# A post-norm decoder layer on one core: a new order of work in the joined cross-attention and routing loop

## The chip, the cores and the metric

The program runs on one NeuronCore of one Trainium2 chip. The metric is the time of one execution on the device, in microseconds (us). Engines are named as in the profile: PE is TensorE's matmuls and PEld its weight loads, DVE is VectorE, ACT is ScalarE, POOL is GpSimd, SP is SyncE, which only issues DMAs.

## The reference, cut to what matters

Batch 64, sequence 64, width 256: 4096 tokens, all fp32.

```python
x = layernorm(x + attn(x))                    # 16 heads, ALiBi, causal
# cross attention: K = V source ctx, scores summed over the batch
A = maximum(abs(masked_scores.sum(0)), 1)     # one matrix for all tokens
O = einsum('hst,bthe->bshe', A, ctx @ Wh)
Y = (O - mean(O)) / sqrt(var(O) + 1e-3) * gamma + beta
x = layernorm(x + (relu(x @ wg) * Y) @ wo)
# feed-forward: 64 experts, top 6 of a softmax router, plus a shared expert
topk_w, topk_idx = top_k(softmax(x @ gate_w.T), 6); topk_w /= sum(topk_w)
routed = sum_k topk_w[k] * (silu(x @ w1[k].T) @ w2[k].T)
g, u = split(x @ shared_gate_up.T, 2)         # 352 columns each
x = layernorm(x + routed + (silu(g) * u) @ shared_down.T)
```

## The kernel before, in words

The 4096 tokens are 32 tiles of 128 (NT = 32). The program has four stages, one after the other: self-attention with the sums of the cross-attention scores (up to 315 us), a joined loop that finishes the cross-attention, norms, routes, runs the shared expert and scatters the rows to pages in HBM (315 to 777 us), the experts page by page (804 to 1284 us), and the combination of the six results with the last norm.

The change lies in the joined loop. Every engine has a list of stages, each with a lag: the helper `tiles` (line 109) walks over steps s, and at step s an engine runs each stage of its list, in the order of the list, for tile s minus its lag. So the list is the order of an engine's queue, written out by hand; semaphores (`ev(name, t)` waits until tile t's event has been counted) tie the engines together. Loops are unrolled four steps deep.

PE's stages (lines 641 to 722), in the order of the list before, with their lags: `c_z_gate` (0), cross-attention product and gate; `ranks` (3), counting of chosen experts; `c_transpose` (1) of the normed group output, line 666; `shared_up` (3), 12 fp32 matmuls of the shared expert's gate and up halves, line 708, in the profile 24 records; `x2_transpose` (2), line 682; `c_project` (1), line 674; `c_out` (0), line 658; `router` (2), line 690; `shared_down` (4), line 718. 

The two norms of the loop share one power on POOL: `pair_rstd` (line 1041) takes for tile t the group norm's variance of t and the second norm's of t - 1, waits for `gn_nm` and `ln2_nm`, makes the power (line 1047) and then mean times power (line 1050, `pair_sh`); ACT applies both (`group_apply`, line 894, and `apply2`, line 904). POOL's queue then has `scatter` (line 1055): six indirect DMAs of the tile with lag 4 (line 1064), which wait for that tile's `ln2_done`, `dest_done` and `tope_done`.

On DVE, `gated` (line 1258) feeds `c_project`; `residual2` (line 1265), `sums2`, `mean2` and `pair_in` (lines 1241, 1242) turn its result into the second norm's statistics; `group_sums` and `group_mean` do the same for the group norm; `shared_gate` (line 1362) and `shared_mul` (line 1368) are the shared expert's gate; `page_...` (lines 1309 to 1349) and `top6...` (lines 1280 to 1303) are the routing, `add_shared` (line 1374) adds the shared expert. On ACT, `x2t_evac` (line 920) copies the transposed row for `router` and `shared_up`, `th_g` (line 949) is the Tanh of the gate half. SP loads `cn` four tiles ahead (line 459).

## Time and profile before

| | us |
|---|---|
| three runs, not profiled | 1398.18, 1401.5, 1402.94 |
| median | 1401.5 |
| the profiled execution | 1399.86 |
| its span | 1398.0 |
| joined loop, 315 to 777 | 462 |
| busy in the span: PE, DVE, POOL, ACT | 1016.2, 785.7, 565.1, 416.3 |

The span is the time from the first to the last instruction that the profile shows; the profiled execution's own time is 1.86 us longer. A record of POOL's indirect DMA is its issue, not its transfer. "Remote" and "another core or an unknown queue" are names for a releaser that the profile could not find among the instructions; this program has one core. The mean granted clock over the span is 0.852, where 1.00 is 2.4 GHz and 0.50 is 1.2 GHz.

### The profile page before, as it was taken

The page shows a single profiled execution, that of the slowest core. Times are in us where ns is not written, and L with a number is a line of the kernel's source. Part 1 is how long each engine was busy: PE and PEld are TensorE (multiplying, and loading weights), DVE is VectorE, ACT ScalarE, POOL GpSimd, SP SyncE. Part 2 cuts the span into 40 slices and gives each one's busy share as a digit, 9 for nine tenths or more (in the row PEclk, how much of TensorE's full clock was granted, in tenths as well). Part 3 has the DMA queues.
Part 4 walks back from the last instruction along what each step waited for, and adds up shares of the span by engine and source line. Part 5 has one row for each costly group of instructions (what it writes and reads, how often), then busy time and mean ns, then how long its engine had stood idle before and what let it go on. Part 6 is the DMA issues. An engine that isn't in the chain of part 4 may idle for free.

```text
span 1398.0 us, 32488 instructions
## 1 busy us (share of the span) xinstructions
PE 1016.2 (73%) x9108; PEld 867.2 (62%) x9108; DVE 785.7 (56%) x2447; ACT 416.3 (30%) x1061; POOL 565.1 (40%) x780
## 2 busy tenths in 40 slices
PE   5699999977776777677765498889888888885000
PEld 4588887867675667566764376678676766673000
DVE  5477777754444444444443365556555555552996
ACT  3355555533232323232321022222222222221121
POOL 0122222221454545454546034456444545553454
PEclk9899999987888878887877589999999999997555
DMA  6455555530221212121132065567555555642994
GB/s 204 146 173 171 171 175 182 180 91 24 76 70 67 70 66 70 66 70 66 67 97 102 24 183 163 166 199 215 179 173 176 184 167 181 195 145 101 300 315 170
DMA packets 136190, 197.13 MB, mean 141 GB/s; under 512 B 18397, under 2 KB 111062, under 8 KB 136152
## 3 DMA queue, kind: packets, MB, share of 16 engines
q1 hardware_dynamic: 68200, 104.04, 24.3%
q10 hardware_dynamic: 47920, 41.09, 10.4%
q0 software_dynamic: 20032, 51.55, 10.1%
q8 instruction: 18, 0.29, 0.1%
q14 instruction: 20, 0.16, 0.0%
HBM read 105.76 MB, written 95.03 MB: 144 GB/s over the span
## 4 chain that ended last, share of the span: by engine, by line
PE 53%; another core or an unknown queue 16%; issue 10%; ACT 7%; DVE 6%; ACTq 4%; DMA 1%; POOL 1%; DVEq 1%; SPq 0%; POOLq 0%
PE psum L746 7%; PE psum L769 7%; PE psum L534 5%; PE psum L718 4%; PE psum L750 4%; PE psum L763 3%; PE psum L779 3%; PE psum L593 3%; PE psum L523 2%; PE psum L547 2%; PE psum L649 2%; PE psum L558 2%; ACTq L969 2%; PE psum L690 1%
## 5 line engine op out<-in xcount | busy, mean ns | idle before, releaser
L1082 POOL DMA_INDIRECT expert_results<-arena,udest x224 | 237.8, 1062 | 278.9 <-issue 227.8
L1064 POOL DMA_INDIRECT expert_rows<-row,dest x192 | 186.9, 973 | 69.1 <-issue 67.9
L1461 DVE COPY arena<-arena 128x896 f32 x224 | 129.4, 640 | 90.1 <-PE psum L750 63.1
L746 PE MATMUL psum<-arena 128*128 128x256 f32 x448 | 129.2, 438 | 60.7 <-ACT arena L983 49.6
L746 PEld LDWEIGHTS psum<-arena 128*128 128x128 f32 x448 | 92.0, 216 | 80.5 <-ACT arena L983 54.0
L1443 DVE COPY arena<-psum 128x512 f32<-128x512 f32 x112 | 72.1, 686 | 82.0 <-remote 45.4
L769 PE MATMUL psum<-arena 128*128 128x128 f32 x896 | 117.5, 285 | 0.0
L769 PEld LDWEIGHTS psum<-arena 128*128 128x128 f32 x896 | 106.7, 195 | 9.9 <-issue 9.9
L1035 POOL TENSOR_TENSOR xnb<-xn,c_bout 128x256 f32<-128x256 f32 x32 | 23.3, 727 | 219.8 <-DVE ln_r L1167 207.7
L690 PE MATMUL psum<-c_wgate,x2t 128*128 128x64 f32 x128 | 28.6, 364 | 107.0 <-ACT x2t L920 98.9
L974 ACT ACTIVATE arena<-psum 128x512 f32<-128x512 f32 x56 | 33.5, 597 | 237.4 <-PE psum L750 160.5
L718 PE MATMUL psum<-c_sdn,arena 128*128 128x256 f32 x192 | 82.6, 595 | 20.2 <-DVE arena L1368 17.8
L1362 DVE SCALAR_TENSOR_TENSOR arena<-arena,psum 128x384 f32<-128x384 f32 x32 | 17.7, 554 | 141.4 <-ACT arena L949 131.9
L690 PEld LDWEIGHTS psum<-c_wgate,x2t 128*128 128x128 f32 x128 | 23.6, 260 | 113.0 <-ACT x2t L920 82.9
L1047 POOL TENSOR_TENSOR pair_rs<-pair_ve,mhalf 128x2 f32<-128x2 f32 x33 | 23.6, 717 | 173.2 <-DVE pair_nm L1242 170.6
L708 PE MATMUL psum<-x2t,c_sgu 128*128 128x128 f32 x768 | 91.4, 276 | 0.0
L708 PEld LDWEIGHTS psum<-x2t,c_sgu 128*128 128x128 f32 x768 | 88.7, 193 | 0.0
L718 PEld LDWEIGHTS psum<-c_sdn,arena 128*128 128x128 f32 x192 | 53.1, 294 | 31.8 <-DVE arena L1368 18.2
L949 ACT ACTIVATE arena<-psum 128x384 f32<-128x384 f32 x32 | 15.7, 490 | 178.7 <-remote 173.3
L534 PE MATMUL psum<-xt,c_wqkv 128*128 128x128 f32 x512 | 68.4, 289 | 0.0
L779 PE MATMUL psum<-c_ident,arena 128*128 128x128 f32 x448 | 60.1, 276 | 11.3 <-DMA arena<-expert_rows 10.1
L750 PE MATMUL psum<-arena 48*128 48x256 f32 x448 | 66.3, 416 | 0.0
(204 smaller groups left out, 2188.8 us busy)
## 6 DMA issues: line engine op xcount, KB each, us to landing
expert_rows<-zeros SPq DMA_DIRECT2D x64, 536.0 KB, 4.8
arena<-expert_rows ACTq DMA_DIRECT2D x224, 134.0 KB
arena<-in_w_experts SPq DMA_DIRECT2D x64, 448.0 KB
arena<-expert_results SPq DMA_DIRECT2D x32, 768.0 KB, 5.2
xn<-in_x SPq DMA_DIRECT2D x32, 128.0 KB, 2.1
cbt<-in_ctx_t SPq DMA_DIRECT2D x32, 128.0 KB, 4.7
cn<-in_ctx SPq DMA_DIRECT2D x32, 128.0 KB
xt<-in_x_t ACTq DMA_DIRECT2D x30, 128.0 KB, 4.7
```

Of the source, the lines that this page charges most:

```text
L534: q = pe.matmul(ps[m], wqkv[:, c, col:col + P], xt[u][:, c, :], start=c == 0, stop=c == 1)
L690: q = pe.matmul(ps_lg, x2t[u][:, c, :], wgate[:, c, :], start=c == 0, stop=c == 1)
L708: q = pe.matmul(ps[:, m, :], sgu[:, c, col:col + P], x2t[u][:, c, :], start=c == 0, stop=c == 1)
L718: q = pe.matmul(ps_sd, sh[u][:, m, :], sdn[:, m, :], start=m == 0, stop=m == SC - 1)
L746: pe.matmul(ps_uy[:, v, :], uhm[:, 4 * u + v, :], uw[:, 4 * u + v, 2 * (IM + IQ) + D:UW], start=True, stop=False)
L750: m = pe.matmul(ps_uy[:, v, :], uhr[own, 2 * u + v // 2, :], uw[own, 4 * u + v, 2 * (IM + IQ):2 * (IM + IQ) + D], start=False, stop=True)
L769: m = pe.matmul(ps_hm[:, v * P:(v + 1) * P], uw[:, 4 * u + v, c * (IM + IQ):c * (IM + IQ) + IM], uxt[:, 8 * u + 2 * v + c, :], start=c == ...
L779: m = pe.transpose(ps_ux[:, v // 2, (2 * (v % 2) + c) * P:(2 * (v % 2) + c + 1) * P], ur[:, 4 * u + v, c * P:(c + 1) * P], ident[:])
L1064: pool.indirect_dma_start(listd, bass.IndirectOffsetOnAxis(ap=dest[u][:, j:j + 1], axis=0), row[u][:], None).then_inc(sem(f"scatter{u}"), 16)
L1082: pool.indirect_dma_start(yd, bass.IndirectOffsetOnAxis(ap=udest[u][:, v:v + 1], axis=0), uy[:, 4 * u + v, :], None, bounds_check=T * K - ...
L1443: m = dve.tensor_copy(uxt[:, 8 * u + 4 * b:8 * u + 4 * b + 4, :], ps_ux[:, b, :].rearrange("p (c n) -> p c n", c=4))
L1461: dve.tensor_copy(uw[:, 4 * u + v, :], ring[:, bass.ds(e & (WS - 1), 1), :].rearrange("p a n -> p (a n)"))\
```

## The change

Four things change in the joined loop. PE's list has a new order and `shared_up` becomes two stages of 12 records each, the gate half and the up half, each of which counts `gu_ready`. ACT's Tanh waits for the gate half alone, and DVE's `shared_mul` waits for both. Mean times power moves from POOL to DVE (`pair_shift`, and one extra call for the last pair), so that POOL waits for the variances alone (`gn_ve`, `ln2_ve`). The lists of ACT and DVE are reordered too, with `add_shared` one step earlier. Two waits on PE change by one tile.

```diff
--- before.py
+++ after.py
@@ -59,7 +59,7 @@
 
 
 PAGE = ("need", "start", "filled", "beyond", "taken", "base", "place", "moved", "top")
-PER_TILE = {"pt_ready": 2, "pt_evac": 2, "w_copied": 4, "h_ready": 2, "page_steps": len(PAGE)}
+PER_TILE = {"pt_ready": 2, "pt_evac": 2, "w_copied": 4, "h_ready": 2, "gu_ready": 2, "page_steps": len(PAGE)}
 IM = 128
 IR = I - IM
 IQ = 64
@@ -669,7 +669,7 @@
             def c_project(k, u):
                 t = 2 * k + u
                 pe.wait_ge(*ev("gt_done", t))
-                pe.wait_ge(*ev("xsh_done", t - 4))
+                pe.wait_ge(*ev("xsh_done", t - 3))
                 for c in range(2):
                     q = pe.matmul(ps_cr, gt[u][:, c, :], wo[:, c, :], start=c == 0, stop=c == 1)
                 q.then_inc(sem("cr_ready"), 1)
@@ -697,29 +697,34 @@
                     q = pe.matmul(ps, w[:], chosen[u][:], start=True, stop=True)
                 q.then_inc(sem("rank_ready"), 1)
 
-            def shared_up(k, u):
-                t = 2 * k + u
-                pe.wait_ge(*ev("x2t_evac", t))
-                pe.wait_ge(*ev("sh_done", t - 1))
-                for g, ps in enumerate((ps_g, ps_u)):
+            def shared_up(g):
+                ps = (ps_g, ps_u)[g]
+
+                def stage(k, u):
+                    t = 2 * k + u
+                    if g == 0:
+                        pe.wait_ge(*ev("x2t_evac", t))
+                        pe.wait_ge(*ev("sh_done", t - 1))
                     for m in range(SC):
                         for c in range(2):
                             col = g * SH + SE[m]
                             q = pe.matmul(ps[:, m, :], sgu[:, c, col:col + P], x2t[u][:, c, :],
                                           start=c == 0, stop=c == 1)
-                q.then_inc(sem("gu_ready"), 1)
+                    q.then_inc(sem("gu_ready"), 1)
+                return stage
 
             def shared_down(k, u):
                 t = 2 * k + u
                 pe.wait_ge(*ev("sh_done", t))
                 pe.wait_ge(*ev("xsh_done", t - 1))
-                pe.wait_ge(*clipped("ln2_sum", t + 3))
+                pe.wait_ge(*clipped("ln2_sum", t + 2))
                 for m in range(SC):
                     q = pe.matmul(ps_sd, sh[u][:, m, :], sdn[:, m, :], start=m == 0, stop=m == SC - 1)
                 q.then_inc(sem("sd_ready"), 1)
 
-            tiles(pe, [(0, c_z_gate), (3, two(ranks)), (1, two(c_transpose)), (3, two(shared_up)), (2, x2_transpose),
-                       (1, two(c_project)), (0, two(c_out)), (2, two(router)), (4, two(shared_down))], ways=4)
+            tiles(pe, [(0, c_z_gate), (3, two(ranks)), (4, two(shared_down)), (0, two(c_out)), (1, two(c_transpose)),
+                       (2, x2_transpose), (3, two(shared_up(0))), (2, two(router)), (1, two(c_project)),
+                       (3, two(shared_up(1)))], ways=4)
 
 
             pe.wait_ge(*paged("taken", NT - 1))
@@ -944,12 +949,12 @@
 
             def th_g(k, u):
                 t = 2 * k + u
-                act.wait_ge(*ev("gu_ready", t))
+                act.wait_ge(*half("gu_ready", t, 0))
                 act.wait_ge(*ev("sg_done", t - 2))
                 act.activation(th[u], ps_g, ACT.Tanh, scale=0.5).then_inc(sem("th_done"), 1)
 
-            tiles(act, [(1, two(group_apply)), (2, apply2), (0, two(z_evac)), (3, two(top6_negative)), (1, two(scale_shift)),
-                        (0, two(w_evac)), (3, two(w_exp)), (3, top6_float), (3, two(th_g)), (2, two(x2t_evac)),
+            tiles(act, [(3, two(top6_negative)), (0, two(z_evac)), (3, two(w_exp)), (3, top6_float), (0, two(w_evac)),
+                        (1, two(group_apply)), (2, apply2), (1, two(scale_shift)), (2, two(x2t_evac)), (3, two(th_g)),
                         (2, two(lg_evac))], ways=4)
 
 
@@ -1010,7 +1015,7 @@
                 pool.dma_start(junk[0:1, 12 + h:13 + h], a["ident"][0:1, h:h + 1]).then_inc(sem(f"y_out{h}"), 16)
             pool.wait_ge(sem("pool_const"), 4)
             credit(pool, "xnb_done", "ln1_rstd", "ln3_rstd", "scattered", "ln1_var", "ln3_var", "ln1_pow", "ln3_pow",
-                   "pair_pow", "pair_done")
+                   "pair_pow")
             pool.wait_ge(sem("first_consts"), n_first)
 
             def rstd(name, col, ways=2):
@@ -1039,15 +1044,12 @@
             pool.wait_ge(sem("filled"), 16 * 2 * NT)
 
             def pair_rstd(t, u):
-                pool.wait_ge(*clipped("gn_nm", t))
-                pool.wait_ge(*ev("ln2_nm", t - 1))
+                pool.wait_ge(*clipped("gn_ve", t))
+                pool.wait_ge(*ev("ln2_ve", t - 1))
                 pool.wait_ge(*ev("gn_done", t - 2))
                 pool.wait_ge(*ev("ln2_done", t - 3))
-                settle(pool)
                 pool.tensor_tensor(pair_rs[u][:], pair_ve[u][:], mhalf[:].to_broadcast([P, 2]), ALU.pow)\
                     .then_inc(sem("pair_pow"), 1)
-                pool.wait_ge(*ev("pair_pow", t))
-                pool.tensor_tensor(pair_sh[u][:], pair_nm[u][:], pair_rs[u][:], ALU.mult).then_inc(sem("pair_done"), 1)
 
             def pair(k, u):
                 pair_rstd(4 * k + u, u % 2)
@@ -1104,7 +1106,7 @@
             credit(dve, "k_evac", "s_read", "max_done", "centred", "rinv_done", "o_norm", "ln1_sum",
                    "ln1_stat", "ln1_mv", "mxt_evac", "gn_stat", "gn_mv", "gt_done",
                    "ln2_sum", "ln2_stat", "ln2_mv", "top_done", "topi_done",
-                   "gn_nm", "ln2_nm", "topm_done", "rest_done", "mask_done", "page_steps",
+                   "gn_ve", "ln2_ve", "gn_nm", "ln2_nm", "pair_done", "topm_done", "rest_done", "mask_done", "page_steps",
                    "rank_read", "dest_done", "sg_done", "sh_done", "xsh_done", "xb_kept", "a_kept", "ux_evac", "w_copied",
                    "udest_done", "uplace_done", "uplaces_done", "ln3_sum", "ln3_stat", "ln3_mv")
             dve.wait_ge(sem("first_consts"), n_first)
@@ -1237,10 +1239,22 @@
                     own = (u + ahead) % 2
                     mv = ln[name, u % 2][2]
                     dve.wait_ge(*ev(name + "_mv", t))
+                    dve.wait_ge(*ev("pair_pow", t + ahead - 2))
+                    dve.tensor_scalar(pair_ve[own][:, col:col + 1], mv[:, 1:2], (GN_EPS, LN_EPS)[col], None, ALU.add)\
+                       .then_inc(sem(name + "_ve"), 1)
                     dve.wait_ge(*ev("pair_done", t + ahead - 2))
-                    dve.tensor_scalar(pair_ve[own][:, col:col + 1], mv[:, 1:2], (GN_EPS, LN_EPS)[col], None, ALU.add)
-                    dve.tensor_scalar(pair_nm[own][:, col:col + 1], mv[:, 0:1], -1.0, None, ALU.mult)                       .then_inc(sem(name + "_nm"), 1)
+                    dve.tensor_scalar(pair_nm[own][:, col:col + 1], mv[:, 0:1], -1.0, None, ALU.mult)\
+                       .then_inc(sem(name + "_nm"), 1)
                 return stage
+
+            def pair_product(t, u):
+                dve.wait_ge(*clipped("gn_nm", t))
+                dve.wait_ge(*ev("ln2_nm", t - 1))
+                dve.wait_ge(*ev("pair_pow", t))
+                dve.tensor_tensor(pair_sh[u][:], pair_nm[u][:], pair_rs[u][:], ALU.mult).then_inc(sem("pair_done"), 1)
+
+            def pair_shift(k, u):
+                pair_product(4 * k + u, u % 2)
 
             def group_sums(k, u):
                 t = 2 * k + u
@@ -1322,6 +1336,8 @@
                 dve.tensor_tensor(fill[:], after[:], need[:], ALU.subtract).then_inc(sem("page_steps"), 1)
 
             def page_beyond(k, u):
+                if isinstance(k, int) and 2 * k + u == NT - 2:
+                    pair_product(NT, NT % 2)
                 dve.wait_ge(*paged("start", 2 * k + u))
                 dve.scalar_tensor_tensor(jump[:], offset[:], float(CHOSEN + P), pages[u][:], ALU.is_ge, ALU.mult)                   .then_inc(sem("page_steps"), 1)
 
@@ -1364,6 +1380,7 @@
             def shared_mul(k, u):
                 t = 2 * k + u
                 dve.wait_ge(*ev("sg_done", t))
+                dve.wait_ge(*ev("gu_ready", t))
                 dve.wait_ge(*ev("sd_ready", t - 2))
                 dve.scalar_tensor_tensor(sh[u], sg[u], 0.5, ps_u, ALU.mult, ALU.mult).then_inc(sem("sh_done"), 1)
 
@@ -1373,13 +1390,13 @@
                 dve.wait_ge(*ev("ln2_done", t))
                 dve.tensor_tensor(slot(xall, t), ps_sd, row[u][:, 0:D], ALU.add).then_inc(sem("xsh_done"), 1)
 
-            tiles(dve, [(5, add_shared), (3, two(page_offsets)), (3, two(page_need)), (1, two(gated)), (3, two(page_start)),
-                        (3, two(page_filled)), (3, two(page_beyond)), (3, two(page_taken)), (3, two(page_base)),
-                        (3, two(page_place)), (3, two(page_moved)), (3, two(page_top)), (3, destinations),
-                        (3, two(shared_gate)), (1, two(residual2)), (0, two(group_sums)), (3, two(shared_mul)),
-                        (1, two(sums2)), (0, two(group_mean)), (2, two(top6)), (0, pair_in("gn", 0, 0)), (1, two(mean2)),
-                        (2, two(top6_only)), (2, two(top6_index)), (1, pair_in("ln2", 1, 1)),
-                        (2, two(top6_out)), (2, two(top6_mask))], ways=4)
+            tiles(dve, [(3, two(page_offsets)), (3, two(page_need)), (3, two(page_start)), (3, two(page_filled)),
+                        (1, pair_shift), (3, two(page_beyond)), (3, two(page_taken)), (3, two(page_base)),
+                        (3, two(page_place)), (3, two(page_moved)), (4, add_shared), (3, two(page_top)),
+                        (0, two(group_sums)), (3, destinations), (0, two(group_mean)), (1, two(gated)),
+                        (0, pair_in("gn", 0, 0)), (3, two(shared_gate)), (2, two(top6)), (1, two(residual2)),
+                        (2, two(top6_only)), (2, two(top6_index)), (1, two(sums2)), (2, two(top6_out)), (1, two(mean2)),
+                        (2, two(top6_mask)), (1, pair_in("ln2", 1, 1)), (3, two(shared_mul))], ways=4)
 
 
             steps = [0]
```

## Rows read from the trace of the kernel before

**Rows 1.** Engines by stage, four tiles: stretch, length, busy us (instructions) PE, PEld, DVE, ACT, POOL; PEclk, DMA, GB/s

```profile
539.00:595.00 56.00, 39.37 (x237) 35.85 (x237) 25.32 (x128) 15.82 (x56) 27.11 (x33) 0.84 0.21 68
```

**Rows 2.** Waits, 371 to 735 us: who waited for whom, us in total, times, longest

```profile
ACT arena L949 <- remote: 144.7, 26, 6.3
POOL pair_rs L1047 <- DVE pair_nm L1242: 131.3, 27, 5.2
```

**Rows 3.** Timeline, one tile, first half: start, us, engine, line, operation, idle before

```profile
538.43 0.72 POOL L1047 TENSOR_TENSOR pair_rs<-pair_ve,mhalf 128x2 f32<-128x2 f32 x1 [4.93 <-DVE pair_nm L1242]
...
540.08 1.03 POOL L1064 DMA_INDIRECT expert_rows<-row,dest  x1 [0.66 <-issue]
...
540.61 0.42 PE L666 MATMUL psum<-c_ident,gn_y 128*128 128x128 f32 x2
...
540.87 2.84 PE L708 MATMUL psum<-x2t,c_sgu 128*128 128x128 f32 x24
...
541.18 0.80 ACT L912 ACTIVATE yt<-psum,c_beta,c_gamma 128x128 f32<-128x128 f32 x2
...
542.36 0.35 DVE L1319 TENSOR_TENSOR_SCAN pages<-ones_f,pages,need 128x64 f32<-128x64 f32 x1
...
543.55 0.38 PE L682 MATMUL psum<-c_ident,row 128*128 128x128 f32 x2
...
543.76 1.03 PE L674 MATMUL psum<-c_wo,gt 128*128 128x256 f32 x4
...
546.49 0.96 POOL L1064 DMA_INDIRECT expert_rows<-row,dest  x1 [0.30 <-issue]
```

**Rows 4.** Timeline, the same tile, from the Tanh to the next indirect DMA

```profile
548.67 0.49 ACT L949 ACTIVATE arena<-psum 128x384 f32<-128x384 f32 x1 [6.04 <-remote]
...
549.49 1.12 PE L690 MATMUL psum<-c_wgate,x2t 128*128 128x64 f32 x4 [4.25 <-ACT x2t L920]
549.67 0.42 DVE L1265 TENSOR_TENSOR ln_r<-psum,xall 128x256 f32<-128x256 f32 x1
550.00 0.42 DVE L1127 BATCH_NORM_STATS2 gn_st<-psum 128x6 f32<-128x256 f32 x1
...
550.34 0.53 DVE L1368 SCALAR_TENSOR_TENSOR arena<-arena,psum 128x384 f32<-128x384 f32 x1
550.40 2.87 PE L718 MATMUL psum<-c_sdn,arena 128*128 128x256 f32 x6
...
550.79 0.42 DVE L1127 BATCH_NORM_STATS2 ln_st<-ln_r 128x6 f32<-128x256 f32 x1
...
551.33 0.15 DVE L1241 TENSOR_SCALAR pair_ve<-gn_mv 128x1 f32<-128x1 f32 x1
...
551.98 0.09 DVE L1297 MATCH_VALUE_LOAD rest<-topm,lg 128x8 f32 x1
...
552.24 0.72 POOL L1047 TENSOR_TENSOR pair_rs<-pair_ve,mhalf 128x2 f32<-128x2 f32 x1 [4.79 <-DVE pair_nm L1242]
552.31 0.20 DVE L1303 TENSOR_SCALAR chosen<-rest 128x64 bf16<-128x64 f32 x1
...
553.04 0.20 POOL L1050 TENSOR_TENSOR pair_sh<-pair_nm,pair_rs 128x2 f32<-128x2 f32 x1
...
553.89 1.03 POOL L1064 DMA_INDIRECT expert_rows<-row,dest  x1 [0.66 <-issue]
```

**Rows 5.** Timeline, before the first scatter

```profile
339.03 2.29 PE L708 MATMUL psum<-x2t,c_sgu 128*128 128x128 f32 x19
...
341.35 0.49 ACT L949 ACTIVATE arena<-psum 128x384 f32<-128x384 f32 x1 [0.92 <-PE psum L708]
```

**Rows 6.** Timeline, end of the joined loop: last indirect DMA, last Tanh

```profile
767.63 0.96 POOL L1064 DMA_INDIRECT expert_rows<-row,dest  x1 [0.30 <-issue]
771.63 0.49 ACT L949 ACTIVATE arena<-psum 128x384 f32<-128x384 f32 x1 [20.27 <-remote]
```

**Rows 7.** Engines by microsecond, columns as rows 1

```profile
548.00:549.00 1.00, 0.00 (x0) 0.00 (x0) 0.00 (x0) 0.33 (x1) 0.00 (x0) 0.50 0.44 137
...
552.00:553.00 1.00, 1.00 (x3) 0.80 (x3) 0.47 (x5) 0.00 (x0) 0.72 (x1) 0.50 0.00 0
```

## The prediction

> **What bounds the kernel now.** I read the table by stage first. In the joined loop four tiles take 56 us and the busiest engine, PE, is busy for 39.37 of them, POOL for 27.11, DVE for 25.32 [rows 1]: none is full, so the loop goes by a cycle of waits. The list of waits names two that lie in every tile: ACT's Tanh waits for a "remote" 26 times in 364 us, 144.7 us in all, and POOL's power waits for DVE, 131.3 us [rows 2]. 144.7 / 26 = 5.6 us of a tile of 14.0.
>
> The timeline of one tile says what this is [rows 3, 4]. The power starts at 538.43 and the next at 552.24: 13.81 us a tile. Six indirect DMAs are issued from 540.08 to 547.45 (546.49 + 0.96). PE's `shared_up` ends at 543.71 (540.87 + 2.84), yet the Tanh, which needs only this, starts at 548.67: 4.96 us later, and 8.59 us after the first indirect DMA. Before the first scatter the same Tanh starts at 341.35, 0.03 us after `shared_up` ends (339.03 + 2.29) [rows 5]. At the end of the loop, where the last tiles' DMAs follow without a pause, it sits idle for 20.27 us and starts 4.0 us after the last issue [rows 6]. I conclude that what PE finishes while a train of indirect DMAs runs is signalled late, mostly when the train is through. I call this the hold. `c_transpose` ends at 541.03, 0.95 us into the train, and ACT uses it at 541.18, so the hold sets in later than that: somewhere between 1 and 3.6 us into the train.
>
> So a tile is: hold, 8.59 us from the first DMA to the Tanh; 3.57 us from the Tanh to the next power (548.67 to 552.24); 1.65 us from the power to the next first DMA (552.24 to 553.89). Sum 13.81.
>
> **The change part by part.** 28 tiles (32, less those before the first scatter and at the end) pay this cycle. I call the end of the hold R.
>
> *Mean times power to DVE.* POOL loses `pair_sh`: 0.20 us and the 0.08 us before it [rows 4]. The 0.66 us of issue before the first DMA stays. From power to first DMA 1.65 - 0.28 = 1.37 us: 0.28 us a tile saved. If part of the 0.66 us ran beneath the 0.72 us power, up to 0.66 more would be saved; the other end is nothing at all, if the issue time is counted from the last wait. I take 0.28, which the rows show. The product itself now stands behind `page_offsets` to `page_filled` on DVE: the scan, 0.35 us [rows 3], and four others of some 0.2 us, 1.2 us in all, where POOL made it 1.0 us after the power's start (552.24 to 553.24). So ACT's `group_apply` comes some 0.6 us later after the power. That costs nothing by itself: its next use is `c_transpose` and then `c_project`, whose result cannot be seen before R anyway. Without the hold it would cost 0.6 us x 28 = 17 us.
>
> *From R to the next power, on DVE.* In the 3.57 us the order is Tanh, `shared_gate`, `residual2`, group sums, `shared_mul`, second norm's sums, small ones, the two variances. The new list puts the group sums (0.34, from 550.00 to 550.34), the group's mean and variance (three small instructions, one of them 0.15 us; about 0.2) and `shared_mul` (0.45, from 550.34 to 550.79) outside this stretch, and puts the match-replace (0.33, from 551.98 to 552.31) and the mask (0.20) inside it [rows 4]. 3.57 - 0.34 - 0.2 - 0.45 + 0.53 = 3.11: 0.46 us saved.
>
> *PE's new order.* No matmul is added or removed. The gate half alone releases the Tanh, but at R both halves are signalled together, so the split is worth nothing while the hold lasts. `shared_down` (2.87 us at the half clock [rows 4]) and `c_out` now stand before `c_transpose`; `router` before `c_project`. With the power at 0: mask and `ranks` let `shared_down` start at about 0.6, it ends at 1.9 to 3.5, `c_out` waits for `group_apply` (power 0.72, product at some 1.5, ACT done at some 2.3) and ends at 3 to 4.3, `c_transpose` at 3.4 to 4.8. The train starts at 1.37, so `c_transpose` ends 2.0 to 3.4 us into it, not 0.95. This is the unknown. Bounds: signalled at once, free; signalled at R, the slow rival below. I take it that it gets through with a delay of 1 to 2 us, because only a few short matmuls then stand between the onset and it, where `shared_up` has 24 records; then `yt` (0.80), `gt`, the copy for `router`, `router` (1.12) and `c_project` (1.03) [rows 3, 4] add up to some 4 us and still end about R, and the tile keeps its 8.59 us.
>
> *Waits and queues.* `shared_mul` waits for both halves; behind it stands the next step's `page_offsets`, and both halves are there at R. `add_shared`, one step earlier, now waits for the `shared_down` of the same step, with `destinations`, the group sums and `gated` behind it on DVE: free if `shared_down` is signalled before the hold. The two waits moved by one tile concern tiles that are long done. SP's load of `cn` follows `c_z_gate` four tiles ahead. POOL's six DMAs per tile stay as they are and wait for nothing new.
>
> **Sum.** 0.28 + 0.46 = 0.74 us a tile, x 28 = 21 us. The profiled execution, 1399.86 us with 1.86 us around its span, becomes 1379; the median stands 1.6 us above it, so 1380. The ends of the unknown prices give 1355 to 1392 for this case.
>
> **Rivals.**
> 1. *Slower: `c_transpose` or `shared_down` is caught by the hold.* Place: the `c_transpose` of each tile, or `add_shared` before `gated`. It decides once `c_transpose` ends so far into the train that its signal waits for R. Then after R come `yt` 0.80, the copy 0.4 (`router` starts 0.82 after the Tanh, with Tanh and copy between), `router` 1.12, `c_project` 1.03 (double at the half clock), and `residual2` to the power 2.1 (549.67 to 552.24 is 2.57, with the edits above): 5.4 to 6.5 us in place of 3.11. A tile takes 8.59 + 5.4 + 1.37 = 15.4 to 16.5 us, 1.6 to 2.7 more; 28 tiles give 1446 to 1477, and fewer if only some tiles are caught. For it: the half clock in the idle stretch and still under the next power and `shared_down` [rows 7], and the margin of a microsecond at best. Against it: the few instructions ahead.
> 2. *No change.* The copy for `router` gets through so late that `c_project` ends about 0.7 us after R and eats the gain: 1400. Beside this, the Trainium skill (Perfetto Trace Analysis, Identifying the Most-Contended Engine) holds that improving a kernel means improving the engine with the highest occupancy. By that rule PE would be the bound, no matmul leaves it, and the time would stay; the 39.37 of 56 us speak against it.
> 3. *Much faster: the hold lets things through.* It would need that fewer records per group (12, not 24) are released during the train. The floor is POOL: 1.37 + 7.37 (train) + 0.3 = 9.0 us a tile, 4.8 less, 1268 us; half of that is 1335.
> 4. The split does what it says but is worthless: part of my forecast.
>
> **Numbers.** Forecast 0.54, rival 1 0.27, rival 2 0.11, rival 3 0.08. A measurement of this kernel can tell about 0.3%, 4 us, from no change. Faster by more 0.62, within 0.11, slower 0.27. The time is the forecast's, 1380. For eight in ten the range must reach into rivals 1 and 3: 1340 leaves out most of the very fast case, 1445 the worse half of the slow one. The forecast's own range is 1355 to 1392.
>
> **What would show it.** Right: period of the power about 13.1 us; no `pair_sh` on POOL, first DMA 1.4 us after the power's start; the first thing that ACT does after R is the Tanh, still some 8.6 us into the train; `residual2` to the power without group sums between; `yt` inside the train. Wrong: `yt` or `gated` idle until R and the period over 15 us (rival 1), `c_project` after R (rival 2), or a Tanh well before the train is through (rival 3). My account of the hold itself falls if the Tanh starts at another distance from the first DMA while PE's work ends at the same point.

## The result, and the profile after

The changed kernel took **1343.9 us** (median of 4 runs, 1338.2 to 1349.0), the kernel before 1399.8 beside it: a ratio of 0.964 [0.961, 0.968], 56 us less. The forecast was 21 us less, 1380: the right sign, and well under half of the size.

The page of the changed kernel, time busy and the chain that ended last:

```profile
span 1347.1 us, 32655 instructions
...
PE 998.0 (74%) x9108; PEld 846.3 (63%) x9108; DVE 789.5 (59%) x2480; ACT 420.1 (31%) x1061; POOL 558.4 (41%) x747
...
PE 54%; another core or an unknown queue 11%; issue 10%; DVE 10%; ACT 6%; ACTq 4%; DMA 1%; DVEq 1%; POOL 1%; SPq 0%; POOLq 0%
```

The chain's "unknown queue", in which the remote waits lie, is 11% (16% on the page of the kernel before). By stage, waits from 371 to 680 us, and four tiles by engine (columns as in [rows 1] and [rows 2]):

```profile
DVE arena L1378 <- ACT arena L954: 117.6, 25, 5.4
ACT arena L954 <- remote: 63.3, 13, 5.2
...
ACT arena L954 <- PE psum L711: 49.5, 12, 4.4
...
POOL pair_rs L1051 <- ACT row L948: 51.9, 13, 4.0
...
POOL pair_rs L1051 <- DVE pair_ve L1243: 48.9, 12, 4.1
```

```profile
452.00:508.00 56.00, 44.20 (x292) 39.48 (x291) 27.64 (x143) 18.09 (x62) 31.19 (x33) 0.92 0.23 80
```

Against [rows 2] the Tanh's remote wait has split in two names (63.3 and 49.5 us), and the power's as well (51.9 and 48.9 where DVE had 131.3). PE works 44.20 of 56 us at a clock of 0.92, where it had 39.37 at 0.84 [rows 1].

One tile of the changed kernel, from the end of the hold to the next train (timeline; columns as [rows 3]):

```profile
500.27 1.04 POOL L1066 DMA_INDIRECT expert_rows<-row,dest  x1 [0.19 <-issue]
...
508.78 0.49 ACT L954 ACTIVATE arena<-psum 128x384 f32<-128x384 f32 x1 [5.10 <-remote]
...
509.77 0.22 DVE L1294 MAX8 top<-lg 128x8 f32<-128x64 f32 x1
509.91 0.41 DVE L1279 TENSOR_TENSOR ln_r<-psum,xall 128x256 f32<-128x256 f32 x1
...
510.51 0.41 DVE L1129 BATCH_NORM_STATS2 ln_st<-ln_r 128x6 f32<-128x256 f32 x1
...
510.90 0.21 DVE L1311 MATCH_REPLACE8 rest<-topm,lg 128x66 f32<-128x66 f32 x1
511.10 0.18 DVE L1136 BATCH_NORM_AGGREGATE ln_mv<-ln_st 128x2 f32<-128x6 f32 x1
511.21 0.19 DVE L1317 TENSOR_SCALAR chosen<-rest 128x64 bf16<-128x64 f32 x1
511.32 0.15 DVE L1243 TENSOR_SCALAR pair_ve<-ln_mv 128x1 f32<-128x1 f32 x1
...
511.72 0.72 POOL L1051 TENSOR_TENSOR pair_rs<-pair_ve,mhalf 128x2 f32<-128x2 f32 x1 [4.03 <-DVE pair_ve L1243]
...
512.63 1.03 POOL L1066 DMA_INDIRECT expert_rows<-row,dest  x1 [0.19 <-issue]
...
515.62 0.52 PE L666 MATMUL psum<-c_ident,gn_y 128*128 128x128 f32 x2
...
516.17 0.81 ACT L917 ACTIVATE yt<-psum,c_beta,c_gamma 128x128 f32<-128x128 f32 x2 [1.75 <-PE psum L666]
...
516.54 0.18 DVE L1136 BATCH_NORM_AGGREGATE gn_mv<-gn_st 128x2 f32<-128x6 f32 x1 [0.17 <-issue]
```

Read it with [rows 3, 4]. First DMA 500.27, Tanh 508.78: the hold is 8.51 us, as it was (8.59). Power 511.72, next DMA 512.63: 0.91 us, where it was 1.65. The bracket `[0.19 <-issue]` stands where `[0.66 <-issue]` stood. `residual2` (ln_r, 509.91) to power: 1.81 us, where it was 2.57. These stretches differ a little from tile to tile, so medians are used below. `c_transpose` (L666, 515.62 + 0.52) ends at 516.14 and ACT uses it at 516.17, 3.5 us into the train: it gets through.

A table of pieces, here and below, holds medians over 29 tiles (worked out from the timelines' rows of POOL, ACT and DVE) and the joined stage, from the first `c_z_gate` to the first matmul that reads the pages taken. The row of PE's order alone, further down, comes from an execution in a slower state, 10 us above its kernel's median, so its joined stage may be a little long.

```
                          power to   first DMA to   residual2   tile   joined
                          first DMA  residual2      to power    sum    stage
before (1399.8)           1.65       9.56           2.73        13.94  461.8
changed (1343.9)          0.91       9.66           1.71        12.28  411.6
```

From the Tanh to the next power, the prediction's own piece, it is 3.73 us before and 2.85 after (medians again).

### The profile page after: what moved, and what is told of

Same layout as the page of the kernel before. It is cut to its first block, busy times and chain, and to the rows that moved or that the text cites. A ratio compares the mean times of both kernels' runs of the same rounds, so it can differ in the third digit from the quotient of the medians.

```text
span 1347.1 us, 32655 instructions
## 1 busy us (share of the span) xinstructions
PE 998.0 (74%) x9108; PEld 846.3 (63%) x9108; DVE 789.5 (59%) x2480; ACT 420.1 (31%) x1061; POOL 558.4 (41%) x747
## 4 chain that ended last, share of the span: by engine, by line
PE 54%; another core or an unknown queue 11%; issue 10%; DVE 10%; ACT 6%; ACTq 4%; DMA 1%; DVEq 1%; POOL 1%; SPq 0%; POOLq 0%
PE psum L751 7%; PE psum L774 7%; PE psum L534 5%; PE psum L711 4%; PE psum L755 4%; PE psum L768 3%; PE psum L784 3%; PE psum L722 3%; PE psum L593 3%; PE psum L547 2%; PE psum L523 2%; ACTq L974 2%; PE psum L558 2%; PE psum L658 1%
## 5 line engine op out<-in xcount | busy, mean ns | idle before, releaser
L711 PE MATMUL psum<-x2t,c_sgu 128*128 128x128 f32 x768 | 102.7, 287 | 0.0
L711 PEld LDWEIGHTS psum<-x2t,c_sgu 128*128 128x128 f32 x768 | 100.8, 205 | 1.7
L722 PE MATMUL psum<-c_sdn,arena 128*128 128x256 f32 x192 | 67.7, 504 | 21.1 <-DVE arena L1385 17.0
L534 PEld LDWEIGHTS psum<-xt,c_wqkv 128*128 128x128 f32 x512 | 62.0, 198 | 6.0 <-issue 6.0
L768 PE MATMUL psum<-arena 128*64 128x128 f32 x896 | 63.0, 284 | 3.2 <-DVE arena L1460 3.2
L768 PEld LDWEIGHTS psum<-arena 128*64 128x64 f32 x896 | 49.2, 139 | 22.4 <-issue 18.9
L1183 DVE TENSOR_TENSOR arena<-psum,arena 128x1024 f32<-128x1024 f32 x32 | 39.2, 1224 | 40.6 <-PE psum L572 40.6
```

What stands on the lines that cost most here:

```text
L534: q = pe.matmul(ps[m], wqkv[:, c, col:col + P], xt[u][:, c, :], start=c == 0, stop=c == 1)
L711: q = pe.matmul(ps[:, m, :], sgu[:, c, col:col + P], x2t[u][:, c, :], start=c == 0, stop=c == 1)
L722: q = pe.matmul(ps_sd, sh[u][:, m, :], sdn[:, m, :], start=m == 0, stop=m == SC - 1)
L768: m = pe.matmul(ps_hr[h * IQ:(h + 1) * IQ, j * P:(j + 1) * P], uw[:, 4 * u + v, c * (IM + IQ) + IM:(c + 1) * (IM + IQ)], uxt[:, 8 * u + 2 ...
```

## The experiments

**Theory A**, from the prediction and the trace after: a tile is the hold, then the stretch to the power, then that to the first DMA; product and DVE's order shorten the two stretches and are paid one for one, PE's order is no part of it. **Rival B:** PE's new order carries the gain. Each expectation names the rival that its run is to tell apart.

The kernels ran on several chips, and **the chips differ**. Each experiment has the kernel before beside it on its own chip, so each ratio holds for its chip; microseconds of different groups are compared only where that is said. Group 1 (first to fourth experiment) and group 2 ran where the kernel before takes 1150 and 1156 us, groups 3 to 5 where it takes 1421, 1396 and 1397.

### Groups 1 and 2: chips on which nothing is held

**Product back on POOL**, all else changed (the cut is shortened; the power waits for the negated means again):

```diff
+ pool.wait_ge(pair_pow, t)
+ pool.tensor_tensor(pair_sh, pair_nm, pair_rs, mult)
- (1, pair_shift)                                    # DVE's list
```

> The changed kernel with mean times power back on POOL, behind the power, and the power waiting for the negated means again. The changed kernel took 1343.9 us, and in its trace the first indirect DMA follows the power by 0.91 us, where it was 1.65 before (28 tiles or so of each). Theory A (the product on POOL is worth its 0.28 us and the issue time of the DMA that stood bare behind it, since each tile is a cycle through power, first DMA, hold, Tanh, power): each tile gets 0.74 us longer, 29 x 0.74 = 21 us, 1365 us; hold still 8.5 us. Rival B (the gain lies in PE's order and the clock that comes with it, the product's place is slack): within 5 us of 1344.

Measured 1154.6 us, ratio 1.001 [0.998, 1.004].

**Product alone** on DVE, in the kernel before (POOL without the product and waiting for the variances alone, as in the diff; DVE's list):

```diff
- (3, two(page_need)), (1, two(gated)),
+ (3, two(page_need)), (1, pair_shift), (1, two(gated)),
```

> The kernel before with nothing changed but mean times power made by VectorE, behind page_need and ahead of gated, and the power waiting for the two variances alone. Theory A: first DMA 0.9 us after the power in place of 1.65, 29 tiles x 0.74 = 21 us less than before, 1379 us. Rival B (the late GpSimd issue was hidden, or the product now delays gated and so c_project by more than it saves): no change, 1396 to 1404.

Measured 1161.9 us, ratio 1.008 [1.005, 1.011]: a little slower. The first DMA still follows the power by 0.91 us, but `residual2` comes 5.9 us behind that DMA, where it is 4.4 in the kernel before on such a chip, and the tile is 9.4 us in place of 9.1 on the mean. What delays `residual2` I didn't separate.

**PE's order and the split alone**, in the kernel before (PE's list and its two waits, the waits of Tanh and `shared_mul`, and `add_shared` as in the diff):

> The kernel before with nothing changed but TensorE's new order and the two halves of shared_up (Tanh on the first half, add_shared one step earlier); product on GpSimd, VectorE's and ScalarE's orders old. Theory A (PE's order is no part of the cycle): 1400, or 1389 if the shorter end of the loop comes from shared_down's place. Rival B (PE's order carries the gain): 1350 to 1375. Rival C (the new order needs VectorE's new one: with gated early and shared_mul in the old place PE stops at c_transpose and at shared_down): slower than before, 1410 to 1440.

Measured 1220.8 us, ratio 1.057 [1.051, 1.064]: slower, as rival C has it.

A time beside a kernel before of 1150 says nothing beside the changed kernel's 1343.9. So here are both on a second chip of that kind, unaltered:

> The changed kernel itself, unaltered, because on the chip of the first four experiments the kernel before took 1150.3 us, not 1399.8, its Tanh came 2.6 us behind the first indirect DMA in place of 8.5, and nothing there compares with the changed kernel. If this chip shows the long hold again (before near 1400): ratio 0.964 again. If it does not (before near 1150): Theory A says a tile is then bound by POOL's own list, 0.91 us from power to first DMA in place of 1.66 and the rest alike, 8.3 us a tile in place of 9.04, so 29 x 0.74 = 21 us under the 1154.6 of the product on POOL, some 1133 us, ratio 0.985; rival B (the product on VectorE comes as late as it saves): ratio 1.00.

> The kernel before, unaltered, for its trace on this chip. Time as that of the runs beside it, ratio 1. With a before near 1150, Theory A expects what the first four showed: no hold, Tanh within 3 us of the first indirect DMA and within a few tenths of the end of shared_up, tiles of 9.0 us. With a before near 1400: Tanh 8.6 us behind the first DMA, tiles of 13.9 us.

The changed kernel took 1138.6 us beside 1155.8, ratio **0.986** [0.984, 0.988]. The kernel before on that chip, around one `shared_up`:

```profile
430.52 1.03 POOL L1064 DMA_INDIRECT expert_rows<-row,dest  x1 [0.66 <-issue]
...
430.85 2.84 PE L708 MATMUL psum<-x2t,c_sgu 128*128 128x128 f32 x24
...
433.73 0.49 ACT L949 ACTIVATE arena<-psum 128x384 f32<-128x384 f32 x1 [0.92 <-PE psum L708]
...
436.95 0.96 POOL L1064 DMA_INDIRECT expert_rows<-row,dest  x1 [0.30 <-DVE pair_nm L1242]
...
437.93 0.73 POOL L1047 TENSOR_TENSOR pair_rs<-pair_ve,mhalf 128x2 f32<-128x2 f32 x1
```

The Tanh starts at 433.73, 0.04 us after `shared_up` ends (430.85 + 2.84 = 433.69) and 3.2 us into the train. No hold. The power starts 0.02 us after POOL is through with the last DMA (436.95 + 0.96 = 437.91): POOL's own list is the tile, 9.07 us. The changed kernel there, the same place:

```profile
443.25 0.96 POOL L1066 DMA_INDIRECT expert_rows<-row,dest  x1 [0.30 <-issue]
...
444.47 0.72 POOL L1051 TENSOR_TENSOR pair_rs<-pair_ve,mhalf 128x2 f32<-128x2 f32 x1 [0.26 <-DVE pair_ve L1243]
...
445.39 1.03 POOL L1066 DMA_INDIRECT expert_rows<-row,dest  x1 [0.19 <-issue]
```

8.54 us a tile: power to DMA 0.92, the train, then `[0.26 <-DVE pair_ve]`. So the product's move pays here as one step of POOL's list, from 9.04 (first experiment) to 8.54 us a tile; by the ratios 1.001 - 0.986 = 0.015, 17 us of 1150.

**`shared_down` last again** on PE, its waits as before, `add_shared` a step later and first on DVE:

```diff
- (3, two(ranks)), (4, two(shared_down)), (0, two(c_out)),
+ (3, two(ranks)), (0, two(c_out)),
- (3, two(shared_up(1)))
+ (3, two(shared_up(1))), (4, two(shared_down))
```

> The changed kernel with shared_down back at the end of TensorE's list, and add_shared back one step later and first on VectorE, its waits as before; all else new. Theory A: in the middle of the loop nothing changes (the held work is shared_up, not shared_down); if the shorter end of the loop (10.8 us of the 56) comes from shared_down's place, that much more than the changed kernel, else within 4 us of it. Rival: shared_down at the head of the list fills TensorE while it would idle; put last it adds its 1.5 to 2.7 us to every tile, 40 us or more.

Measured 1189.8 us, ratio 1.030 [1.026, 1.033]: the rival, 51 us more than the changed kernel.

**PE near its old order** (c_out, c_transpose, both up, x2_transpose, c_project, router, shared_down). The old order whole ends in a deadlock with DVE's new list, so `c_out` stays ahead:

> The changed kernel with TensorE's old order as far as the new order of VectorE's work allows it: c_out, c_transpose, both halves of shared_up together, x2_transpose, c_project, router, shared_down (c_out alone stays ahead). Product, VectorE's and ScalarE's orders new. Theory A (TensorE's order is no part of what sets a tile's time): within 5 us of the changed kernel. Rival B (it carries a large part): over 15 us more.

Measured 1244.2 us, ratio 1.076 [1.073, 1.078]. Theory A's claim for PE's order falls on this chip. With `shared_down` last, PE has nothing to do while it waits for the group norm, and its clock falls (timeline, then engines by stretch, of the run with `shared_down` last; the last row is the changed kernel's):

```profile
447.82 1.09 PE L658 MATMUL psum<-c_wh,zt 128*128 128x128 f32 x4 [2.00 <-ACT gn_y L899]
...
449.56 2.38 PE L711 MATMUL psum<-x2t,c_sgu 128*128 128x128 f32 x12
```

```profile
449.00:452.00 3.00, 3.00 (x19) 3.00 (x17) 1.19 (x6) 1.10 (x4) 2.39 (x3) 0.60 0.34 107
```

```profile
448.00:451.00 3.00, 3.00 (x26) 2.90 (x25) 1.80 (x8) 1.80 (x6) 2.37 (x3) 1.00 0.31 113
```

PE idles 2.00 us before `c_out`; then twelve matmuls of `shared_up` take 2.38 us at a granted 0.60, where the changed kernel takes 1.50 (start 448.10) at 1.00. With 0.55 us of idle time ahead of `c_out` its clock doesn't fall. These 0.9 us are a part of the 1.7 us by which the mean tile is longer (10.26 against 8.56); how the rest divides between the clock and the waiting I didn't work out.

### Group 3: a chip with the hold

> The changed kernel, unaltered, as the measure for the others of this group. With a before near 1150: ratio 0.986 as on the chip before. With a before near 1400: 0.964.

1366.4 us beside 1421.4, ratio 0.959 [0.955, 0.962].

> The changed kernel with mean times power back on POOL, as in the first experiment, now beside the changed kernel on one chip. Theory A: 0.74 us from power to first DMA for each of 29 tiles wherever the tile is a cycle through them: 21 us more than the changed kernel on a chip with the long hold; on a chip without it 9.04 in place of 8.54 us a tile, 16 us more. Rival: the gain is all in the orders, within 5 us of the changed kernel.

1380.2 us, ratio 0.972 [0.967, 0.977]: 13.8 us more than the changed kernel, not 21.

The trace has a likely reason for the smaller loss: the gate's half now gets through sooner. The Tanh starts ahead of the hold's end in 27 of 29 tiles, 7.2 us behind the first DMA (median), where the changed kernel has 8.5.

**The split undone**, the Tanh waiting for both halves:

```diff
- (3, two(shared_up(0))), (2, two(router)), (1, two(c_project)), (3, two(shared_up(1)))
+ (3, two(shared_up(0))), (3, two(shared_up(1))), (2, two(router)), (1, two(c_project))
```

> The changed kernel with the split undone: both halves of shared_up one after the other where the first stands now, ahead of router and c_project, and the Tanh released by both. Theory A on a chip with the long hold: the two halves are signalled at the same point anyway, so within 5 us of the changed kernel. On a chip without it: router and c_project come 1.5 us later (twelve matmuls), the power follows c_project by some 3 us, and the tile has only 0.3 us of slack behind POOL's list, so 1.2 us x 29 = 35 us more. Rival (the split is only for the Tanh): within 5 us on either.

1370.0 us, ratio 0.963 [0.959, 0.967]: 3.6 us more than the changed kernel, not to be told from nothing. Theory A.

**Both halves of `shared_up` last** on PE, the Tanh last on ACT, `shared_gate` and `shared_mul` last on DVE:

```diff
+ (2, two(router)), (1, two(c_project)), (3, two(shared_up(0))), (3, two(shared_up(1)))
```

> The changed kernel with both halves of shared_up behind router and c_project on TensorE, the Tanh last on ScalarE and shared_gate with shared_mul last on VectorE, so that no long group of matmuls and no shared-expert work stands between c_transpose and the next power. On a chip with the long hold (before near 1400): Theory A (only groups of many matmuls are signalled late) expects c_project and router to be signalled within the train, the power right after the last DMA, 9 to 11 us a tile in place of 12.3, 1230 to 1310; the rival (all that ends late in the train is held) expects c_project held too and the time of the changed kernel or more. On a chip without it (before near 1150): the changed kernel's tile is already POOL's list (8.5 us, of which 0.91 + 7.36 is its minimum), so 1130 to 1140, same as the changed kernel or up to 8 us better.

1454.6 us, ratio 1.019 [1.012, 1.027]: 88 us slower than the changed kernel. Theory A's idea that only groups of many matmuls are held falls. The work ahead of `c_transpose` grew, and it was caught (timeline, one tile):

```profile
508.75 1.03 POOL L1066 DMA_INDIRECT expert_rows<-row,dest  x1 [0.20 <-issue]
...
513.05 0.38 PE L666 MATMUL psum<-c_ident,gn_y 128*128 128x128 f32 x2
...
514.53 0.43 DVE L1129 BATCH_NORM_STATS2 gn_st<-psum 128x6 f32<-128x256 f32 x1 [1.48 <-PE psum L658]
...
516.05 0.81 ACT L917 ACTIVATE yt<-psum,c_beta,c_gamma 128x128 f32<-128x128 f32 x2 [3.08 <-remote]
```

`c_transpose` ends at 513.43 (513.05 + 0.38), 4.7 us into the train, and ACT's `yt`, which needs only it, starts at 516.05, 2.6 us late. `c_out` (ended 513.21) is seen by DVE 1.3 us late. So groups of two and four matmuls are held too. In this tile `yt` is let go 7.3 us behind the first DMA; in the 22 other tiles in which ACT waited for it, it is 8.6 to 8.8 us. Then `yt`, `router` and `c_project` come after the hold: 15.57 us a tile. This is the prediction's slow rival with its price (15.4 to 16.5 us), met in a kernel that was built for another question and expected to be faster.

### Group 4: what stands between the end of the hold and the power

> The changed kernel, unaltered, as the measure for this group. Ratio to before 0.959 to 0.964 on a chip with the long hold (before near 1400 or 1420), 0.986 on one without it (before near 1150).

1342.5 us beside 1395.5, ratio 0.964 [0.957, 0.971].

**The second norm first**:

```diff
- (2, two(x2t_evac)), (3, two(th_g)), (2, two(lg_evac))
+ (2, two(x2t_evac)), (2, two(lg_evac)), (3, two(th_g))
- (3, two(shared_gate)), (2, two(top6)), (1, two(residual2)), ... (1, pair_in("ln2", 1, 1)), (3, two(shared_mul))
+ (1, two(residual2)), (2, two(top6)), ... (1, pair_in("ln2", 1, 1)), ..., (3, two(shared_gate)), (3, two(shared_mul))
```

> The changed kernel with the shared expert's activation taken out of the stretch between the end of the hold and the next power: VectorE's shared_gate stands behind the second norm's variance (right ahead of shared_mul), and ScalarE copies the router's logits ahead of the Tanh; TensorE's order is the changed one. In the changed kernel the Tanh (0.48 us) and shared_gate (0.55 us) stand there ahead of residual2. Theory A (a tile on a chip with the long hold is 8.5 hold + 2.84 + 0.91): 0.8 to 1.0 us less per tile, 23 to 29 us under the changed kernel, ratio to before 0.942 to 0.948, unless shared_down comes too late and c_transpose crosses the onset 3.6 us into the train, which gives tiles of 15 us and over 1400. On a chip without the long hold: the tile is POOL's list, same as the changed kernel within 5 us, or slower by the idle time that TensorE gets when shared_down is late.

**1324.3 us**, ratio 0.948 [0.941, 0.954], 18 us under the changed kernel. Its tile:

```profile
501.50 1.03 POOL L1066 DMA_INDIRECT expert_rows<-row,dest  x1 [0.20 <-issue]
...
510.07 0.22 ACT L931 ACTIVATE lg<-psum 128x64 f32<-128x64 f32 x1 [3.38 <-remote]
...
510.26 0.42 DVE L1279 TENSOR_TENSOR ln_r<-psum,xall 128x256 f32<-128x256 f32 x1 [3.26 <-PE psum L674]
...
511.96 0.72 POOL L1051 TENSOR_TENSOR pair_rs<-pair_ve,mhalf 128x2 f32<-128x2 f32 x1 [2.98 <-issue]
...
512.22 0.55 DVE L1378 SCALAR_TENSOR_TENSOR arena<-arena,psum 128x384 f32<-128x384 f32 x1
...
512.87 1.03 POOL L1066 DMA_INDIRECT expert_rows<-row,dest  x1 [0.19 <-issue]
```

The hold ends as before (510.07, 8.57 us after 501.50), but now `residual2` is the first thing that DVE does, and `shared_gate` (512.22) stands behind the power. The tile is 11.38 us. Theory A's term of about 0.9 us a tile is there: 11.45 us on the mean in place of 12.27, 24 us over 29 tiles. The expected 23 to 29 us in all are not: the joined stage is 19 us shorter, because the first tiles took 4 us more and the end of the loop 1 (four executions of the changed kernel differ by 7 us at the first tiles, so that part may be chance).

**Product alone** once more:

> The kernel before with only mean times power moved to VectorE, as in the third experiment, for a chip with the long hold. On such a chip Theory A expects 1.65 to 0.91 us from power to first DMA and all else alike, 0.74 x 29 = 21 us less than before, ratio 0.985; the rival that only the new orders pay expects 1.00. With no long hold 1.008 again, as there: c_transpose stood behind the later product, and the tile is bound by the chain through it.

1375.5 us, ratio 0.988 [0.983, 0.993]: 20 us less than before, where 29 x 0.74 makes 21. Its trace has `residual2` to power 0.24 us shorter too (table below), which Theory A doesn't name. Where nothing is held the same edit lost 0.8%.

### Group 5

> The kernel before with TensorE's new order and the split alone, as in the fourth experiment. On a chip with the long hold (signals of what ends later than 3.6 us into the train come at 8.6): c_transpose stands behind c_out and shared_down, and the product on GpSimd comes late, with scale and shift on the old list behind it; if c_transpose still ends before 3.6 us, about 1.2 us a tile over or under before, 1360 to 1430; if it is caught, tiles of 15 us or more, ratio 1.03 to 1.10 (on a chip without the hold the ratio was 1.057, so Theory A expects 1.03 or more here too). Rival (the order carries the gain alone): 0.97 or less.

1389.3 us, ratio 0.994 [0.990, 0.999]: 8 us less, neither the slowdown of Theory A nor the rival's 0.97. Here the gate's half gets through (timeline, one tile):

```profile
507.49 1.03 POOL L1069 DMA_INDIRECT expert_rows<-row,dest  x1 [0.65 <-issue]
...
509.40 1.50 PE L711 MATMUL psum<-x2t,c_sgu 128*128 128x128 f32 x12
...
511.00 0.49 ACT L954 ACTIVATE arena<-psum 128x384 f32<-128x384 f32 x1 [0.16 <-PE psum L711]
```

The first half ends at 510.90 (509.40 + 1.50) and the Tanh starts at 511.00, 3.5 us into the train. So `shared_gate` is done before the hold ends, and `residual2` comes 8.73 us after the first DMA in place of 9.56. Over the tiles the Tanh starts 4.2 us behind the first DMA (median): here the split does what it says. The only other kernel with the hold in which the Tanh mostly starts ahead of its end is the one with the product back on POOL.

The 8 us are less than its trace would give. Its joined stage is 22 us shorter than that of the kernel before in the first measurement, and the rest of the program 22 us longer (958 against 936). Over the four traces of this group that rest runs from 927 to 958 us, and the kernel before has none on this chip, so what this order gains in the loop alone stays open.

> The changed kernel with shared_down last on TensorE and add_shared one step later, as in the seventh experiment. On a chip with the long hold: at the end of the hold TensorE makes shared_down behind shared_mul, ahead of the next step's z_gate, w and ranks, so offset, page_start and the product come 1.5 to 2.9 us later, c_transpose ends 4.5 to 6 us into the train in place of 3.0 and is held: tiles of 14 us or more, ratio over 1.00. Rival (shared_down's place is free, since all waits for the hold anyway): the ratio of the changed kernel, 0.96. On a chip without the hold 1.03 again.

1346.6 us, ratio 0.964 [0.954, 0.974], the changed kernel's: the rival. And `c_transpose` gets through although it is late:

```profile
500.39 1.03 POOL L1066 DMA_INDIRECT expert_rows<-row,dest  x1 [0.20 <-issue]
...
505.17 0.38 PE L666 MATMUL psum<-c_ident,gn_y 128*128 128x128 f32 x2
...
505.59 0.81 ACT L917 ACTIVATE yt<-psum,c_beta,c_gamma 128x128 f32<-128x128 f32 x2 [0.50 <-issue]
```

It ends at 505.55, 5.2 us into the train, and `yt` starts 0.04 us later. In the run with `shared_up` last it was caught at 4.7 us. So the onset is no fixed time behind the first DMA.

> The version with the second norm ahead of the shared expert's activation again. On a chip with the long hold: ratio 0.948 as before. On one without it: the tile is POOL's list (0.91 + 7.4 us), so the changed kernel's 0.986 within 0.005, or up to 0.01 worse if shared_down comes late and TensorE idles ahead of c_out.

1329.2 us, ratio 0.951 [0.944, 0.958], the same again: 16 us under the changed kernel of this group, which follows.

> The changed kernel, unaltered, as the measure for this group: ratio 0.964 with the long hold, 0.986 without.

1345.2 us beside 1397.3, ratio 0.960 [0.951, 0.970].

The pieces of a tile in the runs with the hold, worked out as above:

```
                          power to   first DMA to   residual2   tile   joined
                          first DMA  residual2      to power    sum    stage
product alone             0.91       9.58           2.49        12.98  436.5
PE's order alone          1.65       8.73           2.73        13.11  439.3
changed (group 4)         0.91       9.65           1.71        12.27  404.3
product back on POOL      1.64       8.90           1.79        12.33  419.6
split undone              0.91       9.92           1.71        12.54  418.6
shared_down last          0.91       9.72           1.73        12.36  405.8
second norm first         0.91       8.80           1.70        11.41  385.3
```

## Why the prediction was right in its sign and wrong in its size

**The cycle was right.** The forecast said that a tile is the hold, then the stretch to the power, then the stretch to the first DMA, and that what falls out of the two stretches is paid in full. The hold stayed at 8.5 us; the second norm ahead of the activation took 0.85 us out of a tile's rest, and the tile became that much shorter. The cycle runs for 29 tiles, not 28.

**Failed: the product's term, 0.28 us.** The trace says 0.74 (1.65 to 0.91). The 0.66 us of issue before the first DMA ran mostly beneath the power once nothing stood behind it: `[0.19 <-issue]` after a power that ends 0.19 us before. I had this as "up to 0.66 more" and took the low end. The product alone, on a chip with the hold, gives 20 us of the 21 that 29 x 0.74 makes. Undone in the changed kernel it costs 14, not 21: the train begins later, and `residual2` comes 8.90 us behind its first DMA in place of 9.65 (medians; the mean tile is 12.54 us, against 12.27 in group 4).

**Failed: the stretch on DVE, 0.46 us.** From the Tanh to the power it went from 3.73 to 2.85, 0.88 less. Taken off were 0.34 + 0.2 + 0.45 = 0.99; added were match-replace and mask, 0.53 us. Of the 0.53 only about 0.1 is to be found, and in another place. The part from `residual2` to the power lost 1.02 us (2.73 to 1.71). The part from the Tanh to `residual2` gained 0.13; there the new list puts the routing's maximum (509.77, 0.22 us) ahead of `residual2`. The prediction left that one out. In the rows after, match-replace starts at 510.90, while the statistics still run (510.51 + 0.41 = 510.92), and the mean and variance at 511.10, 0.18 us behind them. That gap is there without them too: the group norm's aggregate (516.54) stands 0.25 us behind its statistics (515.86 + 0.43 = 516.29), 0.17 of it idle. The mask starts at 511.21, and the variance (511.32) follows the aggregate at its own 0.22 us. Small instructions without a dependence lie in the gaps of a chain of dependent ones and cost it next to nothing here. With both terms right the sum would have been 0.74 + 0.88 = 1.62 a tile, 29 x 1.62 = 47 us; the median tile lost 1.66.

**Not forecast: the end of the loop.** From the last power to the first matmul on the pages taken the kernel before needs 32.1 us, the changed one 21.3. The forecast had no term for it. Before, three trains ran on without a pause and the last Tanh waited for all of them [rows 6]. After (timeline, end of the loop):

```profile
708.47 1.03 POOL L1066 DMA_INDIRECT expert_rows<-row,dest  x1 [0.19 <-issue]
...
722.55 0.96 POOL L1066 DMA_INDIRECT expert_rows<-row,dest  x1 [0.30 <-issue]
...
725.49 0.42 DVE L1391 TENSOR_TENSOR xall<-psum,row 128x256 f32<-128x256 f32 x1 [3.27 <-remote]
725.61 0.49 ACT L954 ACTIVATE arena<-psum 128x384 f32<-128x384 f32 x1 [9.65 <-PE psum L711]
...
726.08 0.17 DVE L1371 TENSOR_SCALAR dest<-top_place 128x6 int32<-128x6 f32 x1
...
727.05 0.96 POOL L1066 DMA_INDIRECT expert_rows<-row,dest  x1 [3.54 <-issue]
...
727.35 1.56 PE L722 MATMUL psum<-c_sdn,arena 128*128 128x256 f32 x6 [0.98 <-DVE arena L1385]
```

`add_shared` (725.49) stands ahead of the last tile's destinations on DVE and is itself held, so POOL has no third train to issue: it pauses for 3.54 us. Two trains are then out, twelve DMAs from 708.47 on, and the hold lets go after 17.0 us. The Tanh starts at 725.61, the destinations are made at 726.08, and `shared_down` with all behind it runs beside the last train. With the product alone the old picture stays (Tanh idle 17.1 us, 30.0 us in all); with PE's order alone, or with `shared_down` last, it is 22, and with the split undone 21.5. So this part belongs to PE's order, and in it neither to `shared_down`'s place nor to the split. Which of its other moves does it I didn't separate.

**The account**, by the two profiled executions: the 29 tiles lose 1.48 us each on the mean (13.77 to 12.29; the medians say 1.66), 43 us; the tiles ahead of them take 4 us more (within the 7 us by which executions of the changed kernel differ there); the end of the loop 11 less. That is 50, the joined stage's 461.8 - 411.6. The executions are 51 us apart and the medians 56. By the experiments the parts taken alone do not add up to the 56: product alone 20, PE's order alone 8, so about 28 of the 56 come only with DVE's new order and with all of it together; that order was not run alone.

**Slow rival (0.27): right as a mechanism, not in this kernel.** Its place is real: it cost 88 us with `shared_up` last. In the changed kernel `c_transpose` ended 2.2 to 3.9 us into the train (median 3.0), where 2.0 to 3.4 was forecast, and wherever ACT waited for it, it was seen within 0.05 us, without the 1 to 2 us of delay that the forecast allowed. That it got through was partly luck: matmuls that ended at 3.1 us were held in the kernel before. **No change (0.11):** wrong; `c_project` comes with the end of the hold, not 0.7 us after. The Trainium skill (Perfetto Trace Analysis, Identifying the Most-Contended Engine) would have had PE, the busiest, as what to improve first. No matmul left PE and 56 us went, out of its idle time (busy 44.20 of 56 us, where it was 39.37); that the time would stay without a matmul less was the prediction's reading, and more than the section says. **Much faster (0.08):** in this kernel the hold let the gate's half through in one tile of 29. On chips without it the tile goes to 8.5 us, nearly all of it POOL's list, below the forecast's 9.0. **The split is worthless:** 3.6 us, right with the hold; without it the split was not undone by itself.

**Failed: "PE's new order is worth nothing".** With the hold it is 8 us alone. Its trace shows two places for a gain, the end of the loop (10 us shorter) and `residual2` (0.8 us a tile earlier), and these are more than the 8 us; the difference is open, as said above. The move of `shared_down` is worth nothing there; by the rival's account, because what it delays waits for the end of the hold anyway. Without the hold the same move is worth 51 us, and the near-old order costs 105.

## What to carry to other kernels

In a loop that turns on a cycle of waits, divide the tile at its signals and price an edit by the piece that it leaves; take off what leaves the dependent chain, but add nothing for small independent instructions that fit its gaps. When an engine waits at one point of every tile, look for work of another stage to put there, and check the granted clock behind it. Have the kernel before run beside every experiment: the same kernel may take 1150 us on one chip and 1400 on another, and an edit can win on one and lose on the other.

## What was unexpected of the hardware

**Only some chips show the hold.** The five groups ran on five chips. On two of them (before 1150.3 and 1155.8 us) matmuls are seen at once all through the trains, and no engine has a remote wait in the middle of the loop; on three (1421.4, 1395.5, 1397.3) and in the first measurement (1399.8) what PE ends a few microseconds into a train of six indirect DMAs is mostly seen 8.5 to 8.8 us after the first one. The joined stage of the kernel before takes 305 us on the one kind and 462 on the other. Another 90 us of the difference lie behind that stage, where the experts' loop has 224 indirect DMAs; how they come about is not worked out here. The hold goes by the number of DMAs. The 8.5 us are 6 x 1.42. At the end of the changed kernel's loop, 12 DMAs without a pause give 17.0 = 12 x 1.42 us (first issue 708.47, `add_shared` 725.49); at the end of the kernel before, 18 give 25.6 = 18 x 1.42 us (746.06, Tanh 771.63). Shorter trains were not tried.

**The hold has gaps.** Of some 440 late signals in the middle of the loops (thirteen traces with the hold; late is more than 0.35 us behind the matmul's end), about 50 came sooner than 8.4 us, most with the product back on POOL and with PE's order alone. They came at 4.2, 5.0, 5.7, 6.4, 7.2 and 7.8 us behind the first DMA, within 0.2: steps of 0.7 us, half of the 1.42. The onset moved, from caught at 3.1 us in the kernel before to free at 5.3 us with `shared_down` last. I don't know what sets it, nor what the chips have different.

**One edit, two signs.** The product alone: 0.988 with the hold, 1.008 without. `shared_down` last: 0.964 (as the changed kernel) and 1.030 (the changed kernel 0.986). The second norm first was measured only with the hold; what it does without it is open.
